# Keys and queries of a two-block attention kernel staged in DRAM with 16, 24 or 8 as the outermost dimension, with seven products and new instruction orders

## The reference

```python
# block 0: one head of 128, then three gated experts
nx = layer_norm(x, gamma, beta)
scores = (nx @ Wq) . (ctx @ Wk) * 128 ** -0.5
evidence = softmax(scores) @ (ctx @ Wv)
combined = [nx, evidence, cond]
x1 = x + sigmoid(gate(combined)) * (sum_e probs_e * expert_e(combined) @ out_w + out_b)
# block 1: 16 heads of 8
q = (ada_ln(x1, cond) @ Wq + bq).reshape(B, 256, 16, 8)
k, v = (ada_ln(ctx, cond) @ Wkv + bkv) in 16 heads of 8
out = x1 + concat_heads(softmax(q k^T / sqrt(8)) v) @ Wp + bp
```

## Time and profile before

| | |
|---|---|
| median of 3 runs | 241.36 us (240.87 to 243.3) |
| the profiled execution, its time | 241.37 us |
| its span, first to last instruction | 239.5 us |
| mean granted TensorE clock | 0.906 of full |
| PE busy | 186.6 us (78%) |
| DVE busy | 141.5 us (59%) |
| ACT busy | 120.3 us (50%) |
| POOL busy | 51.3 us (21%) |
| DMA queue of SP and ACT, share of 16 engines | 15.8% |
| longest shares of the chain that ended last | PE L712 50%, DMA k_st<-k_scr 10% |

### The profile page before, as it was taken

How to read it: one execution, slowest core, us unless ns; L and a number is a source line. 1 busy time by engine, 2 the same in 40 slices (tenths; PEclk the granted TensorE clock), 3 DMA queues, 4 the chain that set the end, 5 groups by cost and what they waited for, 6 DMA issues and landing times.

```text
span 239.5 us, 4440 instructions
## 1 busy us (share of the span) xinstructions
PE 186.6 (78%) x1534; PEld 116.3 (49%) x1538; DVE 141.5 (59%) x386; ACT 120.3 (50%) x263; POOL 51.3 (21%) x81
## 2 busy tenths in 40 slices
...
PEclk9999999999855699996899997599999659999999
...
GB/s 128 344 247 6 5 0 0 18 66 72 118 60 36 89 92 19 37 53 62 20 4 33 4 66 77 54 8 3 28 41 92 55 18 3 45 5 23 4 3 22
DMA packets 10871, 12.32 MB, mean 51 GB/s; under 512 B 1480, under 2 KB 9570, under 8 KB 10466
## 3 DMA queue, kind: packets, MB, share of 16 engines
q1 hardware_dynamic: 10792, 12.03, 15.8%
q10 hardware_dynamic: 58, 0.01, 0.0%
...
## 4 chain that ended last, share of the span: by engine, by line
PE 55%; DMA 14%; DVE 7%; ACT 6%; issue 6%; SPq 6%; POOL 4%; ACTq 0%; DVEq 0%; POOLq 0%
PE ps L712 50%; DMA k_st<-k_scr 10%; PE ps L715 5%; DMA q_st<-mT 4%; SPq L398 3%; ACT probs L663 3%; DVE mparts L1260 3%; SPq L408 2%; POOL cn L505 1%; DVE xn L1244 1%; DVE bias_rows L1022 1%; POOL qr L537 1%; ACT L569 1%; POOL qp L535 1%; POOL kr L522 0%
## 5 line engine op out<-in xcount | busy, mean ns | idle before, releaser
L1260 DVE TENSOR_REDUCE mparts<-ps 128x1 f32<-128x512 f32 x128 | 81.7, 682 | 41.4 <-PE ps L712 41.2
L663 ACT ACTIVATE probs<-ps 128x512 f32<-128x512 f32 x128 | 66.6, 603 | 26.5 <-PE ps L712 26.2
L712 PE MATMUL ps<-k_st,q_st 48*128 48x512 bf16 x128 | 24.3, 415 | 27.6 <-issue 13.5
L712 PE MATMUL ps<-probs,vtile 128*32 128x256 f32 x512 | 34.9, 395 | 0.8 <-ACT probs L663 0.7
L712 PE MATMUL ps<-q_st,k_st 51*128 51x256 bf16 x256 | 23.1, 285 | 10.3 <-DMA q_st<-mT 9.2
L712 PEld LDWEIGHTS ps<-k_st,q_st 48*128 48x128 bf16 x128 | 6.2, 95 | 44.6 <-issue 19.8
L712 PEld LDWEIGHTS ps<-probs,vtile 128*32 128x32 f32 x512 | 14.2, 112 | 13.9 <-ACT probs L663 4.0
L712 PEld LDWEIGHTS ps<-q_st,k_st 51*128 51x128 bf16 x256 | 9.8, 97 | 22.7 <-DMA q_st<-mT 10.3
L630 ACT ACTIVATE tz<-ps 128x512 f32<-128x512 f32 (+1 forms) x16 | 8.7, 544 | 21.7 <-PE ps L712 21.7
L1194 DVE SCALAR_TENSOR_TENSOR hT<-tz,ps 128x512 f32<-128x512 f32 (+1 forms) x16 | 9.9, 617 | 10.0 <-ACT tz L630 9.8
L712 PE MATMUL ps<-nxT,w 128*128 128x256 f32 x48 | 14.3, 380 | 0.0
...
## 6 DMA issues: line engine op xcount, KB each, us to landing
...
```

The costliest lines, as they stand in the source:

```text
L663: A.activation(probs[:, g % 2, j, half * 2 * T:(half + 1) * 2 * T], bank("unit", b, n, side=two), ACT.Exp).then_inc(s["e"], 1)
L712: return nc.tensor.matmul(out, lhsT, rhs, start=start, stop=stop)
L1260: V.tensor_reduce(cells(mparts, g, 0)[:, t, two, u:u + 1], bank("tile", b, n, side=two), AX_X, ALU.max, negate=True).then_inc(s["mx"], 1)
```

## The change

Four things change together.

1. **Layout of the scratch.** `k_scr` was [place, part, side, 8, pair, 512], now it is [place, 16, part, pair, 512], where 16 is side and head column together. `q_scr` joins side and head column as well. So that a partition of the projection is (head column of the pair) x 8 + pair, the projections' columns and biases are permuted: `wk_p` and `wq_p` are permuted copies of the weights (ACT tasks `p9k`, `p9q`), and the bias columns come from permuted rows (`p9a` on ACT, a transpose `P9` on PE, `p9b` on ACT). The value projection is untouched.
2. **Shapes of the transfers.** `k_out` writes 16x8x512 in place of 8x16x512. `q_out` writes one 128x256 block. `k_in` reads rows (column, part) together, 24 rows of 8 KB, or 8 rows. `q_in` reads its 8 rows with a repeat of 3 inside, not outside.
3. **Seven products.** The rows of a side are now 24, 24 and 8 (query part 1 meets key part 2 as well), 56 in place of 48. A batch's `k_in` carry 896 KB in place of 768, its `q_in` 448 KB in place of 384.
4. **The orders** of PE, ACT, DVE, POOL and SP are written anew.

The diff, its order tables left out:

```diff
-ROW_OF = (0, 3 * DH, 5 * DH)
-KR = 6 * DH
+ROW_OF = (0, 3 * DH, 6 * DH, 7 * DH)
+KR = ROW_OF[NP]
...
+        cols_p = sb("cols_p", [P, NR])
+        wk_p = sb("wk_p", [P, P])
+        wq_p = sb("wq_p", [P, P])
...
-        q_scr = nc.dram_tensor("q_scr", (2, NP, 2, DH, NS, T), BF16, kind="Internal").ap()
-        k_scr = nc.dram_tensor("k_scr", (2, NP, 2, DH, NS, S), BF16, kind="Internal").ap()
+        q_scr = nc.dram_tensor("q_scr", (2, NP, 2 * DH, NS, T), BF16, kind="Internal").ap()
+        k_scr = nc.dram_tensor("k_scr", (2, 2 * DH, NP, NS, S), BF16, kind="Internal").ap()
...
+        def by_pairs(view):
+
+            return view.rearrange("r (s x) -> r x s", x=2 * DH)
...
-            return slice(SIDE * two + ROW_OF[i], SIDE * two + ROW_OF[i] + (NP - i) * DH)
+            return slice(SIDE * two + ROW_OF[i], SIDE * two + ROW_OF[i + 1])
...
-                sp.dma_start(k_scr[b % 2, j].rearrange("two d s t -> s (two d) t"), kp[:, j, :]).then_inc(s_kscr, 16)
+                sp.dma_start(k_scr[b % 2, :, j], kp[:, j, :]).then_inc(s_kscr, 16)
...
-                sp.dma_start(q_scr[b % 2, i].rearrange("two d s t -> s (two d) t"), qp[:, i, :]).then_inc(s_qscr, 16)
+                sp.dma_start(q_scr[b % 2, i], qp[:, i, :]).then_inc(s_qscr, 16)
...
-                             k_scr[b % 2, 0:NP - i, two].rearrange("j d s t -> j d (s t)")).then_inc(s_kst[b % 2], 16)
+                             k_scr[b % 2, two * DH:(two + 1) * DH, 0:NP if i < NP - 1 else 1]
+                             .rearrange("d j s t -> (d j) (s t)")).then_inc(s_kst[b % 2], 16)
...
+                one = q_scr[b % 2, i, two * DH:(two + 1) * DH].rearrange("d s t -> d (s t)")
                 sp.dma_start(q_st[places(two, i), b % 2, :, :],
-                             q_scr[b % 2, i, two].rearrange("d s t -> d (s t)").unsqueeze(0)
-                             .to_broadcast([NP - i, DH, NS * T])).then_inc(s_qst[b % 2], 16)
+                             one.unsqueeze(1).to_broadcast([DH, NP, NS * T]) if i < NP - 1 else one).then_inc(s_qst[b % 2], 16)
...
+            def rows_by_pairs():
+                act.wait_ge(s_rows, 16 * 12)
+                A.copy(vec_p.rearrange("r (x s) -> r x s", s=NS), by_pairs(vec_rows[:])).then_inc(s["prep_act"], 1)
...
+            def keys_by_pairs():
+                act.wait_ge(s_wkv, 16)
+                A.copy(wk_p[:].rearrange("r (x s) -> r x s", s=NS), by_pairs(wkv1[:, 0:P])).then_inc(s["prep_act"], 1)
...
+                if b == 0:
+                    act.wait_ge(*of("p9b"))
                 act.wait_ge(*of("kproj", b))
-                A.activation(kf[:], bank("kproj", b), ACT.Identity, bias=cols[:, R_BK:R_BK + 1])\
+                A.activation(kf[:], bank("kproj", b), ACT.Identity, bias=cols_p[:, R_BK:R_BK + 1])\
```

More of the change, by code:

```diff
@@ L53 @@
     "pe": """
[L54 to L83, removed]
-    "act": """
[L85 to L101, removed]
@@ new lines @@
+        P1@0 P2@1 ctxT.0@2 nxT.0@3 P3@4 qm.0@5 P5@6 s0.0.0@7 P4@0 s0.0.1@1 P6@2 p0T.0.0@4 p0T.0.1@3 P5g@5 pc.0@6 P7@0
+        P5b@7 P5c@1 hkvT.0@4 ctxT.1@2 P8@3 P8b@5 hid.0.0@0 nxT.1@6 hid.0.1@7 hid.0.2@1 hid.0.3@4 lgT.0@2 qm.1@3
+        eo.0.0@5 eo.0.1@6 s0.1.0@0 s0.1.1@7 kproj.0@1 P9@4 nxT.2@2 ctxT.2@3 hkvT.1@5 ctxT.3@6 p0T.1.0@0 nxT.3@7
+        p0T.1.1@4 vproj.0@1 pc.1@0 qm.2@4 xqT.0@5 hid.1.0@3 qproj.0@2 hid.1.1@7 hid.1.2@0 hid.1.3@6 lgT.1@5 s0.2.0@4
+        eo.1.0@1 eo.1.1@2 s0.2.1@3 kproj.1@7 p0T.2.0@0 tile.0.0@6+5 qm.3@4 hkvT.2@1 tile.0.1@2+3 tile.0.2@0+6
```

154 lines of the change are left out of this document (104 added, 50 removed).

## The result

The changed kernel takes 210.06 us (median of four runs, 208.53 to 214.19), the kernel before beside it 241.37. The ratio is 0.867, with a 95% interval of 0.856 to 0.878: 13% faster. The profiled execution is the slowest of the four, with the lowest mean clock, and the ratio goes by the three others. The forecast was 198 in a range of 192 to 211. The sign and the range held, but the median lies only 1 us inside the range's upper end, and the likeliest value was 10 to 12 us too low.

The account below looks back on a forecast made before the run. Long scratch reads on few DMA engines bound it: span 239.5 - 35.3 (stops) - 10.15 (clock) + 0.6 + 0.3 (stops left) + 0.5 + 0.5 (orders) = 195.95, plus 1.9 gives 198 us, range 192 to 211.

Parts of the forecast that it names:

- What bounds it: PE stands still 35.3 us at four places because a batch's 12 reads, and what is queued behind them, take long.
- Engines: Scratch reads: the number of DMA engines is short; the new shapes would get 16, 12 and 8.
- The reads' 8.1 us: A batch's load: 6.5 us of issue and movement plus 1.6 landing after the last issue, where it was 21.
- 168 KB at 25 GB/s: A batch's reads: the first engine carries at most 168 KB over at least 8 engines, 6.7 us.
- Stops and clock: PE's stops of 35.3 us shrink to 0.6 plus 0.3, and 10.15 us lost at half clock comes back.
- The prediction's own sign of being wrong: A stop ahead of tile.2.0 or tile.3.0 (A), or no stop, full clock and a span over 202 (B).
- First load, second load, unit.1.0: tile.0.0 at 61.8 waits 0.6 us, not 12.7; the second load's 2.8 and unit.1.0's 9.2 us stops go.
- Seven products and permutation: PE's tiles and units, and four ACT copies: 0 us each, at most 6.7 and 1.8.
- Rival A: Reads reach a common cap of 150 GB/s: 7.5 us more load on the path, up to 2.8 clock; 207 us; chance 0.13.
- Rival B: From tile.0.0 on, the new orders of PE, DVE and ACT wait on each other: 7 us, 205; chance 0.16.
- C: More comes back: half of PE's 5% idling outside the stops was their wake, 4 us less, 194; chance 0.07.
- D: Slower: engine number isn't the limit or the new shape doesn't set it, loads stay at 52 GB/s; about 263; chance 0.04.

Follow-up runs that it names:

- experiment 3: The kernel before with the new scratch layout, transfers and seven products but its old orders (only the permutation's tasks put in): 214.77 us, ratio 0.892.
- experiment 2: The changed kernel's new orders with the old scratch layout, old transfers and six products, plain copies for the permuted ones: 239.13 us, ratio 0.991.
- experiment 1: The changed kernel run again with no edit: 209.47 us (208.67 to 211.46), profiled span 206.9 us.
- experiment 9: Changed kernel, batches 2 and 3: key reads first, each into 96 neighbouring partitions of a buffer nobody reads: 202.23 us, ratio 0.846.
- experiment 4: The changed kernel with six products, its middle reads 16 rows in place of 24: 209.46 us, ratio 0.871.
- experiment 6: Changed kernel, batches 2 and 3: each 24-row read writes every fourth of 96 partitions, in buffers nobody reads: 209.4 us (203.41 to 211.58).
- experiment 10: Changed kernel with batches 2 and 3 issuing six key reads before six query reads, into the usual 24 partitions: 207.84 us, ratio 0.866.
- experiment 12: Changed kernel with own buffers for batch 2's keys and queries, SP's order kept, reads in turn between the two sides: 199.86 us, ratio 0.833.

## Why the prediction was right, and by how much not

- **What bounds it.** Right. The reads' length was the cause of all four stops: with the layout alone 26.6 us came back (experiment 3), with the orders alone 2 (experiment 2). The 9.2 us ahead of unit.1.0 needed both, long reads and mrow behind them: with short reads 2.9 us were left, with the mrow ahead of long reads none.
- **Engines.** The count is right. The Trainium skill ("DMA: Bandwidth & Descriptors", why a DMA increments its semaphore by 16) gave 12 and 8 for the new shapes. The trace agrees: 12.5 engines where keys dominate and 7.7 where only queries are left; with 96 rows it is 15.4 to 15.7. These counts are rough: the share passes 1 in places (1.11 in the start of experiment 1), so it is not a plain count of engines.
- **The reads' 8.1 us: the term that was mis-sized.** Its issue part held (6.3 us for 6.5). Its "1.6 after the last issue" came from a write that had empty queues; behind twelve reads it is 4.3 to 5.95 us. Under it lay "168 KB at 25 GB/s": the rate of an engine when two work. With 12 to 16 at work it is 12 to 17. The count alone doesn't set it: some 7 engines had 9 GB/s each in one window (124.40 in experiment 1) and 21.6 in another (127.00 in experiment 9). The loads are 11.4 to 12.2 us.
- **Stops and clock.** From that one term follow 8.2 us of stops for 0.9, and 4.8 us of lost clock for none: 12.1 us. The span is 206.9 for 195.95, 10.95 more, so the rest of the sum was 1.1 too high, about the 1.0 us set down for the new orders. The prediction's own sign of being wrong came true, a stop ahead of tile.2.0 or tile.3.0, and its clock of 9 throughout did not come. That the time still lay in the range is owed to the range's width.
- **First load, second load, unit.1.0.** tile.0.0's place at 61.78 and the second load's stop of zero are as forecast; unit.1.4's mrow never made a stop.
- **Seven products and permutation.** Zero, as taken, for the products (95 ns a weight load; experiment 4). No run leaves the permutation out; PE's coming to tile.0.0 at 61.78 leaves no room for it.
- **Rival A** comes nearest in its numbers, and 0.13 was too little for it: a load of 10.6 us (measured 11.4 to 12.2), 7.5 us in stops (8.2), 2.8 of clock (4.8), 207 us in all (208.67). As a mechanism it isn't shown. A cap of 150 GB/s is not there: windows with 24 neighbouring partitions reach 172 and 221 (experiments 1 and 6). The spread over 96 shortens a load by 1.7 to 1.8 us (experiments 9, 10), but with 16 engines in place of 12. The Trainium skill's port rule ("SBUF — State Buffer", the DMA port swizzle) gives, as an estimate, 163 GB/s for the 6 ports of 24 neighbours and 218 for the 8 of a whole side. The 221 lie above the first and about at the second. By that rule the spread over 96 could have gone far above 218; it reached 267 in its best window. The sides in turn gave 0.1 to 1.4 us a load.
- **Rival B** fell: with the stops out of the way the same PE, DVE and ACT orders ran in spans of 195.9 to 200.5 (experiment 12), the lowest of them at full clock throughout. That this one meets the forecast's 195.95 to a tenth is in part luck. The sum was about right for a kernel whose loads don't bind.
- **C and D** did not come.

Left open: what holds an engine at 12 to 17 GB/s while many are at work on these reads. A window of experiment 1's start, in which the first inputs and weights come in:

```profile
10.00:15.00 5.00, 5.00 (x21) 2.68 (x19) 2.23 (x5) 2.36 (x8) 3.65 (x5) 1.00 1.11 338
```

It has 338 GB/s, so it is not the core as a whole. Source and shapes of the transfers differ there, and no run here changed the source.
